# A recommendation tower on one core: pair products of the last four tiles in eight halves, with an older tile's first layer between them

## The reference

```python
e = jnp.stack([tbl_0[ids[:, 0]], ..., tbl_49[ids[:, 49]]], axis=1)   # 2048 x 50 x 16
gram = jnp.einsum('bid,bjd->bij', e, e)
z = gram[:, I_IDX, J_IDX]                 # upper triangle, 1225 products
h = jnp.concatenate([z, dense_ctx], axis=1)
h = jnp.maximum(h @ W_top1 + b_top1, 0.0)  # 1241 x 512
h = jnp.maximum(h @ W_top2 + b_top2, 0.0)  # 512 x 256
y = h @ W_top3                             # 256 x 1
```

## Time and profile before

| what | us |
|---|---|
| median of 3 runs | 469.33 |
| lowest, highest | 468.26, 473.47 |
| the profiled execution | 470.18 |
| its span | 468.3 |
| PE busy | 332.6 (71%) |
| POOL busy | 333.8 (71%) |
| DVE busy | 280.0 (60%) |
| ACT busy | 196.3 (42%) |

### The profile page before, as it was taken

How to read it: one execution, slowest core, us unless ns; L and a number is a source line. 1 busy time by engine, 2 the same in 40 slices (tenths; PEclk the granted TensorE clock), 3 DMA queues, 4 the chain that set the end, 5 groups by cost and what they waited for, 6 DMA issues and landing times.

```text
span 468.3 us, 12649 instructions
## 1 busy us (share of the span) xinstructions
PE 332.6 (71%) x5433; PEld 235.5 (50%) x5433; DVE 280.0 (60%) x540; ACT 196.3 (42%) x271; POOL 333.8 (71%) x326
## 2 busy tenths in 40 slices
PE   0567074772979689889686696989587757657876
PEld 0566074661766466657464564666444424233443
DVE  2689499994464798475463988374616172634620
ACT  1436513452445644454444535362475223141321
POOL 5787778777777777777777777777777777774110
PEclk9879556787989979899989898899798979798989
DMA  6994332232222333322133321212111121212010
GB/s 184 416 356 155 118 97 61 76 85 82 57 63 67 104 92 79 110 83 57 20 82 105 81 71 39 61 17 63 36 40 32 42 45 31 61 14 65 8 51 2
DMA packets 24750, 38.71 MB, mean 83 GB/s; under 512 B 8645, under 2 KB 16117, under 8 KB 24565
## 3 DMA queue, kind: packets, MB, share of 16 engines
q1 hardware_dynamic: 13818, 34.43, 22.0%
q0 software_dynamic: 10176, 2.61, 6.4%
q10 hardware_dynamic: 698, 0.85, 0.6%
HBM read 26.79 MB, written 0.13 MB: 57 GB/s over the span
## 4 chain that ended last, share of the span: by engine, by line
PE 24%; POOL 20%; DVE 15%; issue 13%; ACT 11%; SPq 8%; DMA 7%; ACTq 1%; DVEq 0%; POOLq 0%
POOL emb L427 20%; PE hid_ps L731 12%; SPq L366 8%; DVE onehot L469 6%; DMA ids_bc<-ids_dram 5%; PE mid_ps L761 4%; PE look_ps L705 4%; ACT gram L821 3%; PE gram_ps L722 3%; DVE z_both L531 2%; ACT z_both L870 2%; DVE gram L591 2%; DVE turned L583 1%; ACT split L858 1%; DVE w_sb L655 1%
## 5 line engine op out<-in xcount | busy, mean ns | idle before, releaser
L427 POOL DMA_INDIRECT emb<-tbl,gidx x312 | 330.0, 1058 | 97.4 <-issue 92.0
L731 PE MATMUL hid_ps<-w_sb,z_both 127*128 127x512 f16 x528 | 129.6, 393 | 12.1 <-DVE z_both L531 12.1
L705 PE MATMUL look_ps<-parts,onehot 125*128 125x64 f16 x1836 | 82.6, 211 | 65.1 <-DVE onehot L469 49.3
L705 PEld LDWEIGHTS look_ps<-parts,onehot 125*128 125x128 f16 x1836 | 76.5, 110 | 77.4 <-issue 36.0
L821 ACT ACTIVATE gram<-gram_ps 50x784 f32<-50x784 f32 x112 | 91.3, 815 | 43.0 <-PE gram_ps L722 39.9
L469 DVE TENSOR_SCALAR onehot<-ids_bc,rows 125x2048 f16<-125x2048 f16 (+1 forms) x144 | 91.7, 688 | 16.9 <-PE look_ps L705 13.0
L731 PEld LDWEIGHTS hid_ps<-w_sb,z_both 127*128 127x128 f16 x528 | 49.1, 101 | 69.7 <-DVE z_both L531 12.6
L840 ACT ACTIVATE looked<-look_ps 128x1024 f16<-128x1024 f32 (+1 forms) x28 | 26.7, 955 | 84.5 <-PE look_ps L705 84.4
L722 PE MATMUL gram_ps<-turned 32*128 32x100 f16 x2048 | 37.2, 213 | 33.4 <-ACT gram L821 24.6
L583 DVE STREAM_TRANSPOSE turned<-split 128x800 uint32<-128x800 uint32 x32 | 49.5, 1619 | 0.5
L705 PE MATMUL look_ps<-parts_med,onehot 125*128 125x128 f16 x600 | 44.1, 232 | 7.3 <-DVE onehot L469 6.7
(11 more groups left out here) (49 smaller groups left out, 143.0 us busy)
## 6 DMA issues: line engine op xcount, KB each, us to landing
ids_bc<-ids_dram SPq DMA_DIRECT2D x28, 512.0 KB
emb<-tbl,gidx POOLq DMA_INDIRECT x312
z_both<-gram SPq DMA_DIRECT2D x30, 121.0 KB
z_both<-w SPq DMA_DIRECT2D x1, 2816.0 KB
z_both<-gram SPq DMA_DIRECT2D x30, 90.8 KB
z_both<-gram SPq DMA_DIRECT2D x147, 6.2 KB
z_both<-gram SPq DMA_DIRECT2D x30, 60.5 KB
gram<-small SPq DMA_DIRECT2D x2, 512.0 KB, 4.9
```

The costliest lines, as they stand in the source:

```text
L427: pool.indirect_dma_start(emb[:, T % TPC, f, :], None, big[f], bass.IndirectOffsetOnAxis(ap=gidx[:, T, f:f + 1], axis=0)).then_inc(gathere ...
L705: last = nc.tensor.matmul(bank[:, half, at:at + width], onehot[0:TP, at_ring, i, t * TILE:(t + 1) * TILE], moving.rearrange("p i s d -> p ...
L731: return nc.tensor.matmul(hid_ps[:, :], z_parts[0:KP, T % 2, x, k, :], w1_sb[0:KP, k, w, :], start=(i == 0), stop=(i == L1_MM - 1))
```

## The change

Nothing before the last four tiles (T = 12 to 15) is touched. For these:

- The pair products are made in eight halves (`half_dots`). A half is the same loop over pairs of samples with two of the four row groups and thus two of the four banks: 16 matmuls. Halves alternate between the two pairs of banks, so a half waits only for the copies of the half before the last. ACT and DVE copy halves of 392 numbers a partition (`copy_half`). ACT's and DVE's copies count on semaphores of their own.
- Behind each of the eight halves of T = 12, 13, 14 stand two first-layer matmuls of tile T-2, then the other 17 of them, its transposes and its second layer. Before, tile T-1's first layer stood behind `dots(T)`.
- After slot 14 come the first layer of tile 13, its transposes, 6 first-layer matmuls of tile 14 (`EARLY_L1` is 13), tile 13's second layer, 7 more of tile 14, and then tile 15's halves with the other 20 between them.
- DVE takes `split_rows(T)` and `turn(T)` ahead of `split_products(T-2)` and `score(T-3)`. It takes over tile 12's ReLU (`activate`) and its copy (`copy_turned`), and those of tile 14.
- Tile 15's rows are split and transposed in two parts (`last_rows`): 9 of its 19 gathered fields first, and 10 behind the last gather.
- Tile 15's first layer begins when the high part is made, before the low part. Its ReLU is done in two halves of 256 columns, its transposes write two banks, and DVE and ACT copy one half each.

```diff
--- before.py
+++ after.py
...
-LAST_KS = (slice(0, 6), slice(6, ST))
+LAST = NTILES - 1
+FINAL = (NCH - 1) * TPC
+LAST_KS = (range(0, 6), range(6, ST))
+LAST_J = (JS + JM, JS + JM + 5, JJ)
+LAST_FIELDS = 2 * (LAST_J[1] - LAST_J[0]) - 1
+HALVES = 2 * EVACS
+EARLY_L1 = 13
+def halves_of(T):
+    return HALVES * (T - FINAL + 1)
...
+                        if T - LAG < FINAL or e == 0:
+                            pool.wait_ge(gram_done, EVACS * (T - LAG) + e)
+                        else:
+                            pool.wait_ge(half_done, 2 * e)
+                fields = fields_gathered(T)
+                for f in fields:
+                    landed = gathered[T % TPC] if T < LAST or f < fields[LAST_FIELDS] else gathered_last
...
+            def last_rows(x):
+                T, j0, j1 = LAST, LAST_J[x], LAST_J[x + 1]
+                t = T % TPC
+                if x == 0:
+                    dve.wait_ge(gathered[t], rows_gathered(T - TPC) + 16 * LAST_FIELDS)
+                else:
+                    dve.wait_ge(gathered_last, 16 * (NR - LAST_FIELDS))
+                runs = []
+                for a in range(2):
+                    first = max(j0, JS + JM + 1 - a)
+                    f0, f1 = (NM + 2 * (j - JS - JM) - 1 + a for j in (first, j1))
+                    runs.append((emb[:, t, f0:f1 - 1:2, :], split[:, t, first:j1, 0, :, a], split[:, t, first:j1, 1, :, a]))
+                for e, hi, lo in runs:
+                    last = nc.vector.tensor_scalar(hi, e, SCALE, None, ALU.mult)
+                last.then_inc(dve_step, 1)
+                dve.wait_ge(dve_step, 2 * (T + x) + 1)
+                for e, hi, lo in runs:
+                    nc.vector.scalar_tensor_tensor(lo, e, SCALE, hi, ALU.mult, ALU.subtract)
+                nc.vector.tensor_copy(
+                    split[:, t, j0:j1, 2, :, :].rearrange("p j d a -> p j (d a)"),
+                    split[:, t, j0:j1, 0, :, :].rearrange("p j d a -> p j (d a)")).then_inc(dve_step, 1)
+                dve.wait_ge(dve_step, 2 * (T + x) + 2)
+                if x == 0:
+                    dve.wait_ge(half_done, halves_of(T - 2))
+                    j0 = 0
+                src = split[:, t, j0:j1, :, :, :].rearrange("p j s d a -> p j (s d a)").bitcast(U32)
+                for buf, w0 in ((turned, 0), (turned2, DIM)):
+                    out = buf[:, T % 2, :, 2 * j0:2 * j1].bitcast(U32).rearrange("p b j -> p j b")
+                    nc.vector.transpose(out, src[:, :, w0:w0 + WORDS]).then_inc(turned_ready, 1)
+            def copy_half(T, h):
+                if h == 0:
                     dve.wait_ge(packed[T % 2], PIECE_INC * (T // 2))
+                dve.wait_ge(half_done, halves_of(T - 1) + h + 1)
+                out, src = half_evacuation(T, h, 1)
+                nc.vector.tensor_scalar(out, src, 1.0 / (SCALE * SCALE), None, ALU.mult).then_inc(half_by_dve, 1)
+            def activate(T):
+                dve.wait_ge(mlp_done, 3 * T + 1)
+                nc.vector.tensor_scalar(h1[:, :], hid_ps[:, :], 0.0, 1.0 / (WSCALE * ZSCALE), ALU.max, ALU.mult)\
+                    .then_inc(mlp_copied, 1)
...
-            for T in range(first, NTILES):
-                split_products(T - 2)
-                if T > first:
-                    score(T - 3)
+            for T in range(first, LAST):
                 split_rows(T)
                 turn(T)
-                if T == first:
-                    score(T - 3)
-                if T == NTILES - 1:
-                    split_products(T - 1)
-                for e in range(EVACS):
-                    copy_dots(T, e)
-            score(NTILES - 3)
+                split_products(T - 2)
+                score(T - 3)
+                for h in range(HALVES):
+                    copy_half(T, h)
+            activate(LAST - 3)
+            split_products(LAST - 2)
+            copy_turned(LAST - 3, N1, mlp_copied)
+            last_rows(0)
+            score(LAST - 3)
+            split_products(LAST - 1)
+            last_rows(1)
+            for h in range(HALVES):
+                copy_half(LAST, h)
+            activate(LAST - 1)
+            score(LAST - 2)
+            copy_turned(LAST - 1, N1, mlp_copied)
             for i in range(len(LAST_KS)):
                 split_last(i)
-            score(NTILES - 2)
-            score(NTILES - 1)
+            score(LAST - 1)
+            copy_turned(LAST, N1 // 2, hid_by_dve)
+            score(LAST)
...
+            def half_dots(T, h):
+                if h == 0:
+                    pe.wait_ge(turned_ready, 2 * T + (2 if T < LAST else 4))
+                if T == FINAL and h == 0:
+                    pe.wait_ge(gram_copied, TWO * EVACS * T)
+                if T > FINAL or h >= 2:
+                    pe.wait_ge(half_by_act, halves_of(T - 1) + h - 1)
+                    pe.wait_ge(half_by_dve, halves_of(T - 1) + h - 1)
+                for i in range(SLOTS):
+                    b = TWO * (SLOTS * (h // 2) + i)
+                    for buf in (turned, turned2):
+                        for r in range(Q // 2 * (h % 2), Q // 2 * (h % 2 + 1)):
+                            p = slice(32 * r, 32 * r + 32)
+                            last = nc.tensor.matmul(
+                                gram_ps[:, r, i * TWO * NF:(i + 1) * TWO * NF],
+                                turned[p, T % 2, b:b + TWO, :].rearrange("p a m -> p (a m)"),
+                                buf[p, T % 2, b:b + TWO, 0:NF], start=(buf is turned), stop=(buf is turned2))
+                last.then_inc(half_done, 1)
+            def last_mlp():
+                T = LAST
+                pe.wait_ge(mlp_copied, 2 * T - 1)
+                for i, ks in enumerate(LAST_KS):
+                    pe.wait_ge(z_hi, T + 1 + i)
+                    for k in ks:
+                        for w in range(2):
+                            nc.tensor.matmul(hid_ps[:, :], z_parts[0:KP, T % 2, 0, k, :], w1_sb[0:KP, k, w, :],
+                                             start=(k == 0 and w == 0), stop=False)
+                    pe.wait_ge(z_split, T + 1 + i)
+                    for k in ks:
+                        last = nc.tensor.matmul(hid_ps[:, :], z_parts[0:KP, T % 2, 1, k, :], w1_sb[0:KP, k, 0, :],
+                                                start=False, stop=(k == ST - 1))
+                last.then_inc(mlp_done, 1)
+                pe.wait_ge(scored, T)
+                for n in range(N1):
+                    if n % 2 == 0:
+                        pe.wait_ge(mlp_copied, 2 * T + 1 + n // 2)
+                    out = (mid_ps, late_ps)[n // 2]
+                    turn = nc.tensor.transpose(out[:, n % 2, :], h1[:, n * 128:(n + 1) * 128], identity[:, :])
+                    if n % 2 == 1:
+                        turn.then_inc(mlp_done, 1)
+                for n in range(N1):
+                    if n == 0:
+                        pe.wait_ge(hid_by_dve, 1)
+                    if n == N1 // 2:
+                        pe.wait_ge(mlp_copied, 2 * T + 3)
+                    last = nc.tensor.matmul(out_ps, h1_turned[:, n, :], w2_sb[:, n, :],
+                                            start=(n == 0), stop=(n == N1 - 1))
+                last.then_inc(mlp_done, 1)
...
+            def first_part(T, i0, i1):
+                if i0 == 0:
+                    pe.wait_ge(z_split, T + 1)
+                    pe.wait_ge(mlp_copied, 2 * T - 1)
+                for i in range(i0, i1):
+                    last = first_layer(T, i)
+                if i1 == L1_MM:
+                    last.then_inc(mlp_done, 1)
...
-            for g in range(L2_STEP):
-                mlp(first - 2, g)
-            for T in range(first, NTILES - 1):
-                for e in range(EVACS):
-                    dots(T, e)
-                    if e == 0:
-                        mlp(T - 2, L2_STEP)
-                for g in range(L2_STEP):
-                    mlp(T - 1, g)
-            last = NTILES - 1
-            mlp(last - 2, L2_STEP)
-            for e in range(EVACS):
-                dots(last, e)
-                if e in (1, 2):
-                    mlp(last - 1, e - 1)
-            for g in range(2, GROUP_POS):
-                mlp(last - 1, g)
-            for g in range(GROUP_POS):
-                mlp(last, g)
+            for T in range(first, LAST):
+                for h in range(HALVES):
+                    half_dots(T, h)
+                    first_part(T - 2, 2 * h, 2 * h + 2)
+                first_part(T - 2, 2 * HALVES, L1_MM)
+                mlp(T - 2, TURN_STEP)
+                mlp(T - 2, L2_STEP)
+            first_part(LAST - 2, 0, L1_MM)
+            mlp(LAST - 2, TURN_STEP)
+            first_part(LAST - 1, 0, EARLY_L1 // 2)
+            mlp(LAST - 2, L2_STEP)
+            first_part(LAST - 1, EARLY_L1 // 2, EARLY_L1)
+            late = [EARLY_L1 + (L1_MM - EARLY_L1) * h // HALVES for h in range(HALVES + 1)]
+            for h in range(HALVES):
+                half_dots(LAST, h)
```

(46 more changed lines are left out.)

56 lines of the change are left out of this document (33 added, 23 removed).

## The result

The change is slower by some 2%: 481.08 us (median of 4 runs, 477.30 to 481.89) against 470.20 (4 runs, 468.26 to 473.47), a ratio of 1.0201 with a 95% interval of 1.016 to 1.0242. The interval lies wholly above 1; whether the loss is under or over 2% it leaves open. The profiled execution took 480.84 us, its span is 479.0 against 468.3, so +10.7 where the working gave +9.1. PE's busy time rose from 332.6 to 352.6 us with the same 5433 matmuls; the granted clock over the span fell from 0.865 to 0.850.

What follows compares the result with a forecast made beforehand. POOL's gathers set the pace up to 430.22, then a 38.1 us tail. Terms 7.9 + 2.0 − 0.4 − 1.7 + 1.9 − 0.6 gave +9.1 us, 478.4 from 469.33, taken as 478.0; range 470.5 to 482.

Steps and rivals of the forecast that it cites:

- rival A: Last slots: tile 12's and 13's first layers queue on PE behind tile 14's rows; whole sum +9.1 us; chance 0.60.
- A's own bounds: Range given for rival A: 474 to 480.5, from clock penalties of 0 or 4.4 and a half of 0.5.
- rival D: Low clock also falls on tile 13's first layer, or a half costs 0.85: +2 to +4, 480 to 482; chance 0.12.
- 33 matmuls (7.1), 7 insertions (4.0), the clock (1.9): Slot 14, tile 12's first layer on PE between and behind tile 14's halves, from 411.95 to 424.95.
- the gathers end as before, at 428.8: POOL's gathers in the changed kernel: claimed to end at 428.8, not moved by the change.
- The tail: Tile 15's first half to the end: halves +2.0, last copy −0.4, early start −1.7, clock +1.9, ReLU to copies −0.6.
- A half costs a quarter's time: Price of a half's insertion between first-layer matmuls on PE: 0.57 us taken, bounds 0.28 and 0.57.
- Rival B: Halves at 0.3 and the clock up, in slot 14 and tile 15: 470.8, no change; chance 0.19 with its neighbours.
- Rival C: Tail set by last rows, not PE; split rows turned at 431.9: −4.6, 464.7; chance 0.09 with anything else that gains.
- C's terms: Tail terms used for Rival C beside the earlier rows: +2.0, −0.4, −1.7 and −0.6.
- slots 12 and 13 "at nothing": PE's work in slots 12 and 13, about 20 us against POOL's 24.3 a tile: hidden, costing nothing, with 4 us spare.

Runs made afterwards that it cites:

- third set: A wait on POOL's second gather from tile 12 on, in kernel before, change, order without halves or last tile's parts, and all but order: 475.94, 486.64, 481.53, 470.08 us.
- last version: All of the change but its order (halves and last tile's parts kept), no added wait, against the kernel before: 470.07 us against 470.70, ratio 0.9993.
- paced old order: All of the change but its order, with an added wait on POOL's second gather from tile 12 on, against the unpaced kernel before: 470.08 us, ratio 0.9973.
- paced before: The kernel before with an added wait on POOL's second gather from tile 12 on, against itself without it: 475.94 us, ratio 1.0091.
- paced change: The changed kernel with an added wait on POOL's second gather from tile 12 on, against the unpaced kernel before: 486.64 us, ratio 1.0326.
- order alone: The change's loop order on the kernel before, quarters, last tile in one part: 616.18 us (0.9853), again 609.05 (0.9897); with the added wait 481.53 (1.0203).

## Why the prediction was right, point by point

- **The backlog (rival A) is what happened.** Predicted first half of tile 15: 443.7, behind a matmul; measured 445.41, behind a matmul. Tile 13's first layer begins at 431.98 (430.2 predicted), early rows end at 432.0, late ones at 436.3 (432 and 436). The third set shows the mechanism by its place: the same order, with quarters, costs 5.6 us. The last version shows that without the order nothing is lost. By the number alone this was less clear: 481.08 lies above A's own bounds (474 to 480.5) and among those of rival D, and 0.9 us inside the range. Of the 3.1 us over my 478.0, 0.9 is the base, 470.20 for the 469.33 of three runs. The 480.5 itself does not follow from the prices: no block in the rows loses more than 2.2 us, and two of these give 478.6.
- **The mis-sized term: "33 matmuls (7.1), 7 insertions (4.0), the clock (1.9)".** It came to 15.8 us (409.93 to 425.76), not 13.0. The insertions of 0.57 and the matmuls were right. The clock cost 4.7 instead of 1.9, since I took the price from blocks of 33 matmuls (of which the 0.80 covers only one, the block at 402.03). Nothing in the profile before shows the low clock with small products between. My reason for the term failed too. I had PE idle for some six us ahead of slot 14, but it was idle for 0.27: slot 13 had run at 1.2 GHz and ended late. Slot 14 began at 2.4 GHz (0.53 us a half at 408.42) and fell to 1.2 near 412, amid the interleaving. Rival D named half of this ("the low clock also falls on..."), but on tile 13's first layer, which took 7.55 and was not much touched. The loss fell on tile 12's interleaving and on its second layer, which took 3.45 us, 1.5 more than the 1.95 I put.
- **An error the other way hid part of it.** I wrote that the gathers end as before, at 428.8. They ended 1.9 us earlier (last one at 425.99 for 427.88), and tile 14's rows came at 404.01 for 405.88. From those rows to tile 15's first product I had 37.8 us and it took 41.4. That the backlog starts with the rows, so that earlier rows move all of it, was in the sum; that they would be earlier was not. So +10.7 for +9.1 is close by luck: 3.6 us too little behind the rows, and 1.9 too much ahead of them. The rewritten waits did not bring the 1.9: from 350 us on no gather of either profile starts more than some 0.3 us behind the end of the one before. When tile 13's gathers begin, the change is 0.5 us ahead (354.72 for 355.21), when nothing that was changed has run yet. The other 1.4 lie in single gathers that took longer than the usual 0.94 us, six before (1.16 to 1.63 us) and four in the change (1.01 to 1.53). The longest begin while DVE makes a low part, as here in the change:

```profile
408.18 1.69 DVE L565 SCALAR_TENSOR_TENSOR z_both<-z_both 127x704 f16<-127x704 f32 x2
409.17 1.53 POOL L461 DMA_INDIRECT emb<-tbl,gidx  x1 [0.30 <-issue]
```

  Before, tile 13's low part (421.32) met a gather so too (422.27, 1.55 us). In DVE's new order it came at 426.39, behind the start of the last gather. No run tests what stretches them.
- **The tail, term by term.** From the first half to the last: 7.62 for 7.7. Last copy 0.57. Its end to ACT's landing 7.9, as predicted. First layer 0.99 behind the landing for 0.89. The last first layer took 9.04 us for 7.29, +1.75 where I put +1.9; its first 12 matmuls took 375 ns each (4.50 us). ReLU to the end of the second layer in halves 3.5 for 4.1: −0.6. All told 33.6 us for 32.5: +1.1, predicted +1.2.
- **A half costs a quarter's time.** Taken as 0.57, measured 0.57. Of the Trainium skill's rule ("TensorE: Matmul & The Clock Gate", section "Measured speedup vs the span model"), by which two tiles less would shorten a pack by some 8 ns and a half by 64 ns, the rows show nothing: 0.53 us for 32 or for 16 matmuls, and the next matmul starts 0.47 us behind the start of a quarter (439.37 to 439.84, before) and 0.46 behind that of a half (445.41 to 445.87). Here the trace does not bear the rule out.
- **Rival B fell** in both its parts: halves were not cheap and the clock didn't stay up. **Rival C fell** in the change, where DVE waits 9.76 us for PE. Its point, that split rows bring the first product forward by 2.6 us where PE waits for them (434.5 to 431.9), is borne out by the paced old order, 1.7 us behind the last rows for 4.3. From the first product to the end the paced old order takes 31.1 us, where C's terms give 32.5 + 2.0 − 0.4 − 1.7 − 0.6 = 31.8. (The 34.9 of the paced before holds 2.4 us that the kernel before hasn't: its first copy stood behind a low part, and its next matmuls ran at the low clock.) So C was right about the parts and wrong about the order that brought them. My slots 12 and 13 "at nothing": slot 13 with its low clock ran to 408.1 (second layer 406.15 + 1.99), where the next rows were turned at 408.35. It was hidden, but with 0.3 us to spare, not with 4.

## What to carry to other kernels

Work that is ready should stand in an engine's program ahead of work that waits for the slowest stage. Here 33 ready matmuls stood behind products whose rows came at the gathers' pace; the engine first idled (6.48 us ahead of slot 13, 8.43 ahead of slot 14 in the paced change), then had a backlog when only it counted. The idle stretch costs twice, once as idle time and once in what follows at half clock. With halves and two matmuls between them that second part was longer here than with quarters and four (6.5 against 2.9 us in slot 14, both paced), one execution of each. Splitting the last tile's steps is worth what the wait it sits on is worth, so look at what ends just beside it (here PE's second layer, 0.1 us from the product's start) before counting the gain.

## What the runs showed of the hardware

- TensorE stayed at 1.2 GHz through 17 us in which it was busy for 16.38 (granted 0.51). It had been idle for 6.48 us ahead. The same mixture that started behind other matmuls held 2.4 GHz in slot 12 (granted 1.00 over 17 us). These are the change's rows of the two slots:

```profile
362.74 0.53 PE L830 MATMUL gram_ps<-turned 32*128 32x100 f16 x16
363.20 0.61 PE L871 MATMUL hid_ps<-w_sb,z_both 127*128 127x512 f16 x2
...
384.12 0.85 PE L830 MATMUL gram_ps<-turned 32*128 32x100 f16 x16 [6.48 <-DVE turned L620]
...
395.32 0.85 PE L830 MATMUL gram_ps<-turned 32*128 32x100 f16 x16
396.10 1.03 PE L871 MATMUL hid_ps<-w_sb,z_both 127*128 127x512 f16 x2
```

  It also fell from 2.4 to 1.2 GHz near 412, amid the interleaving, after waits of 0.78, 0.69, 0.27 and 0.98 us. What the fall hangs on is open.
- The kernel before took 470.20, 472.06 and 470.70 us in three of the five sets of runs, and 626.26 and 618.00 in two, on other chips. On those two, the edited versions show waits that the profile puts down to a remote releaser; the kernel before itself was not profiled there. The order alone came out at 0.9853 and 0.9897 there; on the first kind, with the added wait, at 1.0203, of which the wait alone makes 1.0091. Without the wait it was never timed on the first kind. What these waits are, no run here shows.
- A gather that begins while DVE makes a low part takes longer in both profiles: 1.53 us at 409.17 in the change, 1.55, 1.60 and 1.63 at 422.27, 400.39 and 379.73 before, where most take 0.94. What the two share was not tested.
